# An attention kernel in which TensorE makes every second head's outer scores one slot earlier, between the two halves of a batch of value products

## What is computed

```
x = x + attn(layernorm(x))          # 16 heads of 8 numbers; key j counts for query i where |i - j| <= 128
x = x + ffn(layernorm(x))           # batch norm, scores against product keys, best 8 of 1024 experts per head
attn: p = softmax(q k^T / sqrt(8), masked);  out = (p v) w_proj^T
```

## Time and profile before

| | |
|---|---|
| median of three runs | 1668.57 us (1667.78 to 1672.3) |
| the profiled execution, time | 1663.86 us |
| its span, first to last instruction | 1662.1 us |
| attention, read from the trace | to about 650 us |
| one step of the attention, c = 3 to 14 | 39.07 us, the same from step to step |

### The profile page before, as it was taken

One profiled execution on the slowest core, in us unless ns is written; L12 is line 12 of the kernel. 1 busy time (PEld: TensorE's weight loads), 2 busy tenths in 40 slices (PEclk: granted clock), 3 DMA queues, 4 the chain that ended last, 5 costly groups with the idle time before them and its releaser, 6 DMA issues.

```text
span 1662.1 us, 33309 instructions
## 1 busy us (share of the span) xinstructions
PE 1474.0 (89%) x10762; PEld 1019.5 (61%) x10762; DVE 1476.8 (89%) x4616; ACT 1314.8 (79%) x1805; POOL 1271.8 (77%) x1547
## 2 busy tenths in 40 slices
PE   5899999999999999788888888888888888888877
PEld 3455555555555554366767667677676776767766
DVE  4999999999999985389999999999999999999997
ACT  1376666666666666579999999999999999999995
POOL 1165555565655555399999999999999999999992
PEclk9799999999999999989999999999999999999999
DMA  6344554444445541100000000000000000000000
GB/s 160 86 109 108 121 112 111 112 105 112 114 111 113 111 102 45 51 1 20 1 20 20 1 20 20 7 14 20 20 1 20 20 2 20 20 7 14 14 7 7
DMA packets 73630, 86.40 MB, mean 52 GB/s; under 512 B 9872, under 2 KB 63760, under 8 KB 68752
## 3 DMA queue, kind: packets, MB, share of 16 engines
q1 hardware_dynamic: 72840, 82.70, 20.5%
q10 hardware_dynamic: 616, 1.57, 0.5%
HBM read 58.30 MB, written 25.95 MB: 51 GB/s over the span
## 4 chain that ended last, share of the span: by engine, by line
POOL 21%; ACT 13%; DVE 10%; issue 8%; PE 7%; DVEq 0%; ACTq 0%; POOLq 0%
POOL SUM L861 21%; DVE W L1091 7%; ACT E L984 6%; PE WT L1158 4%; ACT L901 1%; ACT L900 1%; PE MB L1101 1%; ACT W L944 1%; PE MB L1104 1%; DVE SMALL L1037 1%; ACT SIM L894 1%; DVE M8Y L1020 1%; ACT GE L900 0%; ACT GE L905 0%; ACT GE_first L900 0%
## 5 line engine op out<-in xcount | busy, mean ns | idle before, releaser
L861 POOL TENSOR_TENSOR SUM<-SIM 128x1024 f32<-128x1024 f32 x480 | 899.7, 1931 | 30.5 <-DVE W L1091 26.5
L1158 PEld LDWEIGHTS WT<-idf,W 128*128 128x128 f32 x4096 | 478.6, 147 | 210.4 <-issue 127.6
L1091 DVE SCALAR_TENSOR_TENSOR W<-SUM,SMALL,E 128x1024 f32<-128x1024 f32 x448 | 560.5, 1280 | 43.4 <-ACT E L984 43.0
L1158 PE MATMUL WT<-idf,W 128*128 128x128 f32 x4096 | 544.8, 284 | 56.4 <-DVE CT L1071 38.0
L278 POOL TENSOR_SCALAR_AFFINE_SELECT PT<-PT 128x128 f32<-128x128 f32 (+1 forms) x1024 | 337.0, 355 | 254.3 <-ACT PT L389 220.8
L984 ACT ACTIVATE E<-SUM,NB 128x1024 f32<-128x1024 f32 x448 | 495.6, 1116 | 20.4 <-DVE W L1091 17.7
L448 DVE CUSTOM_DVE_ANT_0 SY<-SY,bandf 128x384 f32<-128x384 f32 x512 | 273.1, 573 | 0.0
L389 ACT ACTIVATE PT<-TX 128x512 f32<-128x512 f32 x256 | 153.1, 598 | 113.8 <-PE TX L583 113.6
L469 DVE TENSOR_REDUCE mx<-SX 128x2 f32<-128x512 f32 x256 | 174.3, 681 | 51.1 <-PE SX L565 51.0
L391 ACT ACTIVATE PT<-TY 128x768 f32<-128x768 f32 x256 | 207.5, 810 | 3.8
L611 PE MATMUL PV<-PT,V 128*32 128x384 f32 (+1 forms) x2048 | 165.2, 441 | 0.8 <-POOL PT L278 0.7
(11 more groups left out here) (135 smaller groups left out, 1901.2 us busy)
## 6 DMA issues: line engine op xcount, KB each, us to landing
Q<-q_parts SPq DMA_DIRECT2D x288, 64.0 KB
K<-k_parts SPq DMA_DIRECT2D x90, 192.0 KB
q_parts<-qp SPq DMA_DIRECT2D x16, 384.0 KB, 2.4
k_parts<-kp SPq DMA_DIRECT2D x15, 384.0 KB, 2.4
xin<-in_x SPq DMA_DIRECT2D x16, 256.0 KB, 3.2
xres<-in_x SPq DMA_DIRECT2D x16, 256.0 KB, 9.4
x<-X SPq DMA_DIRECT2D x16, 256.0 KB, 2.2
x2T<-X2T SPq DMA_DIRECT2D x16, 256.0 KB, 2.1
```

The lines of the kernel that those rows point to most:

```text
L861: return eng.tensor_tensor(SUM[(q * FH + h) % RING][:, :].rearrange("p (i j) -> p i j", i=NK), sx, sy, ALU.add)
L1091: nc.vector.scalar_tensor_tensor(out=W[h % WRING][:, :], in0=SUM[(k * FH + h) % RING][:, :], scalar=TOP[q][:, h, TOPK - 1:TOPK], in1=E[(n ...
L1158: o = pe.matmul(WT[:, e, :], W[h % WRING][:, e * P:(e + 1) * P], ident[:, :], is_transpose=True, start=(h == 0 and e % 4 == 0), stop=(h == ...
```

## The change

The function `scores` is cut into `scores_outer` and `scores_inner`. At the head of an odd slot, and of slot 0, both are called as before. At the head of the other even slots only the inner scores are made: the outer scores of that head have been made in the odd slot before, between the two portions of the values. The last slot's values are left whole, since the next head belongs to another step.

```diff
-        def scores(t, c, h):
+        def scores_outer(t, c, h):
...
             if c > 0 or h > 0:
                 pe.wait_ge(S["outer_maxima"], n - 1)
...
+        def scores_inner(t, c, h):
...
                 if 0 <= c < SEQS:
-                    scores(t, c, h)
+                    if h % 2 or h == 0:
+                        scores_outer(t, c, h)
+                    scores_inner(t, c, h)
...
-                for g, (sl, ds_) in enumerate(VSLOT):
-                    for half_ in range(2):
-                        if h == sl + 2 * half_ and 0 <= c - ds_ < SEQS:
-                            values(t - ds_, c - ds_, g, (2 * half_, 2 * half_ + 1))
+                portions = [(ds_, g, 2 * half_) for g, (sl, ds_) in enumerate(VSLOT) for half_ in range(2)
+                            if h == sl + 2 * half_ and 0 <= c - ds_ < SEQS]
+                for ds_, g, j in portions:
+                    values(t - ds_, c - ds_, g, (j,))
+                if h % 2 and h < H - 1 and 0 <= c < SEQS:
+                    scores_outer(t, c, h + 1)
+                for ds_, g, j in portions:
+                    values(t - ds_, c - ds_, g, (j + 1,))
```

More of the change, by code:

```diff
@@ L544, in _, with tile_scores @@
         pe.wait_ge(S["v_pads_set"], 5)
-        def scores(t, c, h):
-            b, n = c % 2, t * H + h + 1
+        def tile_scores(c, h, out, i, k0, k1, clear=True, done=True):
+            b = c % 2
+            return pe.matmul(out, Q[b][0:KQ, h, i * P:(i + 1) * P], K[b][0:KQ, h, k0 * P:k1 * P],
+                             start=clear, stop=done, skip_group_check=True)
+        def scores_outer(t, c, h):
+            n = t * H + h + 1
             if h == 0:
@@ L552, in scores @@
                 pe.wait_ge(S["heads_8_15_loaded"], 192 * (t + 1))
-            def tile(out, i, k0, k1, clear=True, done=True):
-                return pe.matmul(out, Q[b][0:KQ, h, i * P:(i + 1) * P], K[b][0:KQ, h, k0 * P:k1 * P],
-                                 start=clear, stop=done, skip_group_check=True)
             if c > 0 or h > 0:
@@ L561, in scores @@
                 pe.wait_ge(S["k_rest"], 1)
-            tile(SX[:, 0, :], 0, 0, 2, done=False)
-            tile(SX[:, 1, :], 3, 2, 4, clear=False, done=False)
+            tile_scores(c, h, SX[:, 0, :], 0, 0, 2, done=False)
+            tile_scores(c, h, SX[:, 1, :], 3, 2, 4, clear=False, done=False)
             pe.matmul(SX[:, :, :].rearrange("p j n -> p (j n)")[:, P:3 * P], idb[:, :], bandb[:, :],
                       start=False, stop=True, skip_group_check=True).then_inc(S["outer_scores"], 1)
+        def scores_inner(t, c, h):
+            n = t * H + h + 1
             for e, i in enumerate((1, 2)):
@@ L569, in scores @@
                     pe.wait_ge(S["inner_maxima"], 2 * n - 3 + e)
-                tile(SY[:, e, 0:3 * P], i, i - 1, i + 2).then_inc(S["inner_scores"], 1)
+                tile_scores(c, h, SY[:, e, 0:3 * P], i, i - 1, i + 2).then_inc(S["inner_scores"], 1)
         def scoresT(t, c, h):
```

## The result

The changed kernel takes 1699.89 us (1699.08 to 1706.67), the kernel before 1668.17 in the same comparison: a ratio of 1.0198, 95% interval 1.0179 to 1.0218. It is slower by 32 us; 1696 was forecast. The profiled executions are 1699.67 and 1663.86 us, 36 apart, since the one of before lies 4 us under its median.

The account below looks back on a forecast made before the run. Neither VectorE nor TensorE alone was taken to set the step; TensorE's terms summed to 1.91 us more a step, 22.9 us over twelve steps plus 5.2, so 1668.6 + 28 = 1696 us, range 1675 to 1708.

Parts of the forecast that it names:

- What bounds the kernel: In the attention, VectorE idles 2.2 us a step for outer scores, TensorE waits too; neither engine alone sets the step.
- The rival in which VectorE sets the step: TensorE hides the additions in its waits, VectorE's idle time goes: 1636 us, half of it 1652; chance of faster 0.07.
- Price of a moved product: Each odd slot with a split batch grows by 0.33 + 0.21 = 0.54 us on TensorE, 3.78 us a step.
- The estimate of 0.11 us from the drain: Cost of shape changes per split batch by the skill page's drain of about 128 cycles; the rows' 0.21 was used instead.
- Given back: Slots 4, 6 and 14 return 0.33 us each, slot 2 0.11; 8, 10 and 12 nothing: 1.10 us a step.
- Waits that go: TensorE's waits for VectorE in slots 3, 9, 11 and 13 vanish as VectorE runs ahead: 1.68 us a step.
- Waits that come: TensorE waits mid-values for VectorE's outer maxima, 0.62 us in slot 1 and 0.29 in slot 5: 0.91 a step.
- The sum: TensorE's costs and gains added over all slots: 3.78 - 1.10 - 1.68 + 0.91 = 1.91 us more a step.
- The other steps: The 19 split batches in c = 1, 2 and 15, priced like those of the alike steps: 5.2 us.

Follow-up runs that it names:

- e6: Kernel before, with outer scores made one slot earlier in slots 3, 5 and 13 alone, behind the whole batch of values; ratio to before 1.0005.
- e1: Changed kernel, but the early outer scores stand behind both portions of the values, so no batch is split; ratio to the kernel before 1.0011.
- e3: Kernel before plus a zero-weight product 128 columns wide between the two portions of the values in odd slots up to 13; ratio to before 1.0166.
- e4: Kernel before plus a zero-weight product 32 columns wide between the two portions of the values in odd slots up to 13; ratio to before 1.0026.
- e5: Changed kernel, but the outer scores of head 2 stay at the head of slot 2, so slot 1 is not split; ratio to the kernel before 1.0200.
- e2: Changed kernel, but the early outer scores stand ahead of both portions of the values, so no batch is split; one execution, 1742 us.
- f1: Kernel before, with VectorE's norm of X2 moved to slots 3 and 9 and TensorE's turn of X2 to slot 10; 1655.29 us, ratio 0.9922.
- f2: As f1, plus outer scores one slot earlier behind the whole batch in slots 3, 5 and 13; 1650.69 us, ratio to the kernel before 0.9903.

## Why the prediction was right

The sign, the size of the whole (31.7 us of median where 28 were forecast) and the mechanism in the main were right: the outer scores pay a change of shape in each split batch, and most even slots can't give their time back. The range 1675 to 1708 holds 1699.89. One step was wrong, that TensorE's delays add up over all the slots of a step, and that the sum came out near in spite of it was luck.

- **What bounds the kernel.** That neither engine alone sets the step was right, and e6 shows what follows from it: VectorE's 2.2 us of idle time a step could be moved, but not won. The rival in which VectorE sets the step ends with e1.
- **Price of a moved product.** 0.54 forecast, 0.57 read. The 0.21 for going in and out, taken from the one entry and the one exit that the trace of before shows, is 0.22 in e3 against e4; the rest is the first pass after the second entry, which is a little longer (319.01 to 319.36 in slot 1, 0.35, where 384 columns else take 0.32). The Trainium skill, TensorEngine Tiling (Array Packing), section Key Properties, says that a change of tiling mode drains the array and a change of tile doesn't: e3 and e4 agree in the time, with 0.22 us and nothing up to the next portion; what the array does in it no run shows. The estimate of 0.11 us from the drain in the Trainium skill, TensorE: Matmul & The Clock Gate, section Step-by-step: what each phase is for, was half of what a pair of changes costs here.
- **Given back.** 1.10 forecast, 1.07 read. That slots 8, 10 and 12 would give nothing was right: from TX to TY it stays 1.78 us in slots 8 and 10, and in slot 12, behind a copy, 1.98 before and after.
- **Waits that go.** 1.68 forecast, 1.61 read in slots 3, 9, 11 and 13. But the reason was half wrong. In slots 9, 11 and 13 VectorE does get ahead. In slot 3 the wait went because slot 1 made TensorE later, which is no gain: e5 has it back. Slot 1 has a wait for VectorE in its inner scores as well, which the forecast left out; 0.09 of it went.
- **Waits that come.** The term that was mis-sized: 0.91 forecast, 1.18 read. Slot 1 is 0.73 and not 0.62, slot 5 is 0.28 and not 0.29, and slot 7, where I counted none, has 0.17: there too VectorE is held by a projection's copy (line 511), and the longer first portion doesn't quite cover it.
- **The sum** came out near by luck, because its two errors of reading are nearly equal. The 1.16 us of slot 1 (0.54 and 0.62) were counted as a cost, the 1.03 of slot 3 as a gain; both lie in VectorE's stretch, where TensorE is made to wait anyway. Taken by stretches the cost is: six split batches from slot 3 on, 3.42, less 0.97 given back in slots 4, 6 and 14, less 0.66 of waits in slots 9, 11 and 13, plus 0.45 in slots 5 and 7, together 2.24 us, where the second stretch grew by 2.27; the rest up to 2.43 is VectorE's stretch, 0.16 longer (below). By the forecast's way of adding, e5 would have lost 1.2 us a step less than the changed kernel, and e1 would have been 0.4 under before; they were 0.13 less and 0.15 over.
- **The other steps.** 19 batches were priced at 5.2 us. The attention's last exponential starts at 680.79 us before (the attention lasts to there and not to about 650) and at 717.21 after, 36.4 us later, and twelve steps make 29.2 of it, so these steps and the start took 7.2. A part of that may be the granted clock at the start, which differs from run to run.

## What to carry to other kernels

Before moving an operation earlier for one engine's sake, look at what shape of work it lands between on the engine that makes it: here two more changes of the array's shape cost two thirds of the operation itself, and a trace of the kernel before shows that price wherever the two shapes already meet. An engine's idle time is worth something only if the next thing it waits for also comes earlier; follow it one wait further. And a sum of delays over an engine's slots holds only within the stretch that this engine sets: find the hand-over points in a step (a wait that returns when the engine gets faster marks one), and take work out of the stretch that ends there.

## What the runs showed of the hardware

Some of VectorE's small operations get longer beside GpSimd's masks. Timeline of VectorE and GpSimd, changed kernel, slot 10:

```profile
342.15 0.82 POOL L278 TENSOR_SCALAR_AFFINE_SELECT PT<-PT 128x256 f32<-128x256 f32 x2 [0.15 <-ACT PT L391]
```

```profile
342.18 0.52 DVE L444 TENSOR_TENSOR mp<-rm,mp 32x128 bf16<-32x128 f32 x1
```

Line 444 took 0.52 us under these two masks, and 0.28 in the kernel before in slot 3, with no mask beside it; its mean went from 316 to 442 ns with the change. From 100 to 660 us of all thirteen traces this operation took 0.27 to 0.28 us in each of 122 places without a mask; where masks ran beside it throughout, it took 0.35 to 0.36 under the small ones (128x128) and 0.46 to 0.52 under the large ones (128x256). Line 438, which is as small but reads one of its two inputs from PSUM, took 0.27 to 0.28 with and without. One half of the norm of X2 in slot 2 went from 0.59 to 0.80 us; before, small masks ran beside it, and with the change large ones. The change moved nothing on either engine, it only made them meet otherwise, and VectorE's stretch grew with it. No run moves the masks alone, so that the 0.16 us of that stretch come from there and nowhere else is not shown.

The granted clock fell in each step of e2 from c = 3 to 14, behind a wait of TensorE of 1.2 us in slot 1. It did not fall behind e2's waits of 0.9 us in slot 7, nor in the same steps of the changed kernel, where the wait in slot 1 is 0.7. And at the start of the attention, step c = 1, it differs from run to run of whatever kernel. Windows from 74 to 114 us, f1 and then f2:

```profile
74.00:114.00 40.00, 38.84 (x266) 21.38 (x266) 31.93 (x101) 25.88 (x44) 21.86 (x65) 0.84 0.39 88
```

```profile
74.00:114.00 40.00, 38.32 (x316) 20.59 (x313) 37.04 (x116) 28.87 (x51) 25.50 (x77) 1.00 0.48 103
```

f1's profiled execution ran at the lower level for a part of that stretch (0.84 on the mean) and got through 266 of TensorE's products where f2 got through 316. From copy to copy on the line of V, step c = 1 took 39.1 us in f1 and 34.7 in f2, while the later steps differ by 0.06: the step length tells kernels apart more finely than the total.
